# Cross-attention and expert block: another order of scores, maxima and weighings within each group

## The chip, the cores and the metric

The kernel runs on one core of one Trainium2 chip. The metric is device time of one execution in microseconds, the median of several runs. Before the change three runs gave 823.15 us in the median (822.39 to 824.36).

## The reference

The input is `x` (4 batches, 512 tokens, 256 channels) and a context of 4 x 1024 tokens. Three things are computed:

```
x = x + cross_attention(layernorm(x), context, context, mask)   # 16 heads of 16 channels, rope on q and k,
                                                                # scores / 4, masked keys -10000, softmax, @ w_o.T
x = x + ffn(layernorm(x)), where ffn is
    h + attention over the 4 batch entries of a token (causal softmax, 4 kv heads), then
    + sum over the top 2 of 8 experts of gate * (gelu(y @ w1) @ w2), y = layernorm(h)
```

The change touches only the first of these, the cross-attention: for each batch and head, 512 queries against 1024 keys, `softmax(q k / 4) v`.

## The kernel before

The program has three blocks, one after the other: cross-attention (`cross_attention`), the second attention with routing (`second_block`), and the experts (`experts_block`). Only the order of work in the first is changed.

The cross-attention is cut into 16 *quads* (four heads of one batch) and each quad into 8 *key tiles* of 128 keys. A quad and a key tile make a *group*; there are 128 groups. What a group has to do:

- four *scores* S0 to S3 (L966), one for each head: a matmul of 128 keys by 512 queries into a bank. ScalarE takes the exponential of each (L616) into a buffer of probabilities;
- one *weighing* (L981): four heads' probabilities times the values, which add up in the bank `values` over the 8 key tiles. The weighing of group g-1 stands inside group g;
- some *maxima* for the next quad (L928, then VectorE's reduction L757). The softmax subtracts a maximum of each query row, so the scores are computed once before with queries as rows, two matmuls of 512 columns each into a *wide* slot, and reduced by VectorE. A quad has 16 of them, spread over some 7 groups of the quad before, so a group has two in most cases, sometimes one or three or none;
- *jobs*: `nm` (VectorE puts a quad's 16 maxima together), `mxt` (TensorE turns them, L933, ScalarE copies them to `mxp`, L610, and SyncE moves them into the query stack by DMA, L387, so that the score matmul subtracts them), `xn` and `xT` (the normalised input of the next batch and its transpose), `q`, `k`, `v` (projections), `rope` and `c` (GpSimd), `out` (transpose of a quad's weighed sum and division, L938), `oT` and `oP` (transpose and output projection).

`attention_order` gives every job and maximum a time; the whole part of the time is its group. `steps_of` (L91) then writes out the order within each group, and each engine goes through that one list and takes what is its own. So the list sets the program order of TensorE, ScalarE and VectorE at once. From group 116 on (`g >= late`) there are no maxima, and the list is another.

Two rings hold the results of TensorE. Scores, `q`, `k`, `v` and `mxt` take three banks (`narrow`) in turn, by L280: a score waits for the exponential (or the copy) of the third one before it in that ring. Maxima, `xT`, `out`, `oT` and `oP` take two wide slots in turn: each waits until VectorE is through with the one before the last. A weighing waits for all four exponentials of its group:

```
pe.wait_ge(exp_done, 4 * g + 4)
```

An engine carries out its list in order. What waits holds up all that stands behind it on its engine.

The heads of a quad lie in pairs: S0 and S2 use rows 0 to 63 of the array, S1 and S3 rows 64 to 127 (`r = HALF * (hq % 2)`). Of a maximum's two matmuls, the first uses rows 64 to 127 and the second rows 0 to 63.

Of the kernel before, what the change touches and what calls it, by code (L numbers as in the profile page):

```python
# [35 lines left out]
def lead(quad):  # L36
    return 3 + 0.25 * max(quad - 5, 0)
# [8 lines left out]
def attention_order():  # L46
# [12 lines left out]
    for t in range(1, B):  # L59
        g = 32 * (t - 1)  # L60
        timed += [(g + 5.8, ("xn", t)), (g + 7, ("xT", t)), (g + 8.5, ("q", t, 0)), (g + 10, ("q", t, 1)), (g + 10, ("rope", t, 2))]
        timed += [(g + x, ("v", t, n // 2, n % 2)) for n, x in enumerate((11.5, 13.5, 15, 16.5))]
    for t in range(2, B):
        g = 32 * (t - 2)
# [5 lines left out]
    for b in range(B - 1):  # L70
        g = 32 * b + 32
# [5 lines left out]
    def when(g):  # L77
        return begins[int(g)] + (g - int(g)) * lengths[int(g)]
# [5 lines left out]
    for quad in range(1, QUADS):  # L84
        first, last = when(max(8 * (quad - 1) - lead(quad - 1), 0)), when(8 * quad - lead(quad))
# [5 lines left out]
    def steps_of(g):  # L91

        here = [j for t, j in timed if int(t) == g]
        tops, rest = [[j for j in here if (j[0] in ("max", "nm")) == is_max] for is_max in (True, False)]
        if g >= late:
            return [("job", ("pair", g)), ("score", 4 * g + 2), ("score", 4 * g + 3), ("weigh", g - 1)] + [("job", j) for j in rest]
        first, later = rest[:1], rest[1:]
        early = tops[:1] if len(tops) > 2 else []
        tops = tops[len(early):]
        steps = [("score", 4 * g)] + [("job", j) for j in early + first] + [("score", 4 * g + 1)] + [("job", j) for j in tops[:1]] + [("score", 4 * g + 2)]  # L100
        steps += [("weigh", g - 1)] * (g > 0) + [("score", 4 * g + 3)]
        for n in range(max(len(tops) - 1, len(later))):
            steps += [("job", j) for j in tops[1 + n:2 + n] + later[n:n + 1]]
        return steps

    steps = [steps_of(g) for g in range(GROUPS)]
    after = [("moments", 0), ("warm", GROUPS), ("out", QUADS - 1), ("warm", GROUPS + 1), ("oT1", B - 1), ("warm", GROUPS + 2), ("oP1", B - 1, 0), ("tile0", 0), ("oP1", B - 1, 1), ("warm", GROUPS + 3)]
    after += [("root0", 0), ("again0", 0), ("root0", 1), ("rates0", 0)]
# [1835 lines left out]
```

## Time and profile before

| | |
|---|---|
| median of three runs | 823.15 us |
| the profiled execution, first to last instruction | 808.3 us |
| TensorE matmul busy | 706.0 us (87%) |
| VectorE busy | 557.3 us (69%) |
| ScalarE busy | 485.6 us (60%) |
| GpSimd busy | 355.8 us (44%) |
| exponentials (L616), of one score each | 488, mean 601 ns |
| reductions of maxima (L757) | 256, mean 1223 ns |

The profile is of one execution, so its span and the median of the runs are not the same thing; launch and end lie outside the span. "Busy" counts a matmul from its start to its modelled end, so that two matmuls in different halves of the array overlap and a TensorE that is busy 87% of the time can still be short of its peak. In the rows further down a time is microseconds from the start of the span. The timeline puts equal instructions that follow each other into one row (x2, x8); its start is that of the first.

### The profile page before, as it was taken

How to read it: one execution, taken by the hardware profiler on the slowest of the kernel's cores; microseconds unless marked ns; L12 is line 12 of the kernel's file. 1: busy time of each engine (PE TensorE's matmuls, PEld its weight loads, DVE VectorE, ACT ScalarE, POOL GpSimd, SP SyncE). 2: the span in 40 equal slices, each digit the busy share in tenths (PEclk: the TensorE clock that was granted, in tenths of full speed). 3: DMA queues.
4: the chain of work that ended last, by engine and by line, in shares of the span. 5: the costliest groups of instructions: out<-in, count | busy, mean ns of one | idle time of the engine just before them, and what ended most of it. 6: DMA issues, size and time to landing. Idle time of an engine off the chain costs nothing. (4 is left out here: it accounts for less than half of the span.)

```text
span 808.3 us, 13262 instructions
## 1 busy us (share of the span) xinstructions
PE 706.0 (87%) x4318; PEld 425.8 (53%) x4318; DVE 557.3 (69%) x924; ACT 485.6 (60%) x940; POOL 355.8 (44%) x262
## 2 busy tenths in 40 slices
PE   3246899999899999899999899888978889999996
PEld 2242434443344443435334333276767778999986
DVE  5949777778777778778878884248996515555553
ACT  2010556777576778567766678856655136676673
POOL 4964605358006277005749991000035723544444
PEclk9775689999999999999989999999998799999999
DMA  9676264868655666114777872039925646633321
GB/s 258 213 224 165 84 240 124 229 155 271 206 158 173 176 187 239 58 45 119 224 260 262 276 273 79 1 93 358 344 53 135 256 108 141 120 35 40 33 32 20
DMA packets 59718, 130.71 MB, mean 162 GB/s; under 512 B 8869, under 2 KB 26309, under 8 KB 58197
## 3 DMA queue, kind: packets, MB, share of 16 engines
q1 hardware_dynamic: 33364, 72.86, 27.6%
q0 software_dynamic: 16848, 35.95, 17.6%
q10 hardware_dynamic: 9440, 21.06, 9.0%
q8 instruction: 37, 0.61, 0.3%
q14 instruction: 29, 0.23, 0.1%
HBM read 80.80 MB, written 69.39 MB: 186 GB/s over the span
## 5 line engine op out<-in xcount | busy, mean ns | idle before, releaser
L757 DVE TENSOR_REDUCE mx<-wide 128x2 f32<-128x1024 f32 x256 | 305.6, 1223 | 89.0 <-PE wide L928 88.4
L616 ACT ACTIVATE probs<-narrow 128x512 f32<-128x512 f32 x488 | 267.3, 601 | 94.4 <-PE narrow L966 92.6
L966 PE MATMUL narrow<-qst,kst 51*128 51x512 f32 x488 | 182.9, 464 | 4.2 <-ACT probs L616 3.5
L928 PE MATMUL wide<-kst,qst 49*128 49x512 f32 x512 | 159.7, 476 | 21.4 <-DVE mx L757 9.4
L966 PEld LDWEIGHTS narrow<-qst,kst 51*128 51x128 f32 x488 | 78.9, 190 | 147.3 <-ACT probs L616 94.7
L981 PE MATMUL values<-probs,vaug 128*17 128x512 f32 x1024 | 139.2, 616 | 1.4 <-ACT probs L616 0.8
L1735 POOL DMA_INDIRECT out<-res,token x39 | 61.2, 1569 | 91.7 <-DMA out<-res,token 60.2
L928 PEld LDWEIGHTS wide<-kst,qst 49*128 49x128 f32 x512 | 68.6, 198 | 43.7 <-DVE mx L757 28.0
L462 POOL TENSOR_TENSOR turn_b<-turn_a,tab 128x1024 f32<-128x1024 f32 x10 | 24.2, 2420 | 115.3 <-ACT turn_a L610 114.8
L1267 POOL DMA_DIRECT2D out<-xt x4 | 5.5, 1376 | 108.1 <-DVE xt L1462 108.1
L1760 ACT ACTIVATE h_hi<-narrow 128x512 fp32r<-128x512 f32 x39 | 23.3, 598 | 42.2 <-PE narrow L1840 42.2
L1786 DVE TENSOR_TENSOR h_lo<-narrow,h_hi 128x512 fp32r<-128x512 f32 x39 | 27.0, 692 | 23.3 <-ACT h_hi L1760 23.3
L1274 POOL DMA_INDIRECT list_rows<-lists,rows_to x32 | 32.2, 1008 | 17.9 <-DVE rows_to L1532 9.1
L981 PEld LDWEIGHTS values<-probs,vaug 128*17 128x17 f32 x1024 | 17.1, 96 | 42.9 <-issue 27.6
L457 POOL TENSOR_SCALAR keep<-keep 128x512 f32<-128x512 int32 x7 | 13.7, 1960 | 52.9 <-ACT turn_a L610 42.8
L1782 DVE TENSOR_TENSOR y_lo<-y_full,y_hi 128x256 fp32r<-128x256 f32 x39 | 16.6, 426 | 29.0 <-ACT y_hi L1747 29.0
L1747 ACT ACTIVATE y_hi<-wide,lncol 128x128 fp32r<-128x128 f32 x78 | 36.3, 465 | 0.0
L1746 ACT ACTIVATE y_full<-wide,lncol 128x128 f32<-128x128 f32 x78 | 35.8, 459 | 0.1
L610 ACT ACTIVATE vaug<-narrow 128x512 f32<-128x512 f32 x16 | 9.6, 599 | 34.5 <-PE narrow L828 34.5
L1831 PE MATMUL wide<-w_hi,y_hi 128*128 x78 | 28.2, 442 | 0.1
L1591 PE MATMUL narrow<-ident 128*128 128x128 f32 x172 | 24.9, 314 | 3.7 <-PEq L1900 2.1
L610 ACT ACTIVATE mxp<-narrow 8x512 f32<-8x512 f32 x16 | 9.3, 580 | 30.9 <-PE narrow L933 30.8
(281 smaller groups left out, 1310.4 us busy)
## 6 DMA issues: line engine op xcount, KB each, us to landing
list_rows<-in_w ACTq DMA_DIRECT2D x56, 342.0 KB, 5.5
kst<-k_pieces SPq DMA_DIRECT2D x14, 784.0 KB
k_pieces<-turn_a SPq DMA_DIRECT2D x16, 512.0 KB, 5.2
w_hi<-w_hi SPq DMA_DIRECT2D x16, 512.0 KB, 11.0
w_lo<-w_lo SPq DMA_DIRECT2D x16, 512.0 KB, 11.8
turn_a<-in_w POOLq DMA_DIRECT2D x11, 512.0 KB, 5.7
w_hi<-turn_b POOLq DMA_DIRECT2D x11, 512.0 KB, 3.0
w_lo<-turn_a POOLq DMA_DIRECT2D x11, 512.0 KB, 4.6
```

Source lines behind the costliest of these rows:

```text
L616: nc.scalar.activation(probs[:, n % NP, :], score_bank(n), ACT.Exp, scale=DK ** -0.5).then_inc(exp_done, 1)
L757: last = nc.vector.tensor_reduce(mx[quad % 2][:, qt, :, hp, kh], slot[:, :, :], axis=AX.X, op=ALU.max)
L928: last = nc.tensor.matmul(slot[:, i, :], qst[u % 3][r:r + R_MAX, h, P * qt:P * qt + P], kst[u % 3][r:r + R_MAX, h, 512 * kh:512 * kh + 512 ...
L966: nc.tensor.matmul(score_bank(n), kst[u % 3][r:r + R_ALL, h, P * kt:P * kt + P], qst[u % 3][r:r + R_ALL, h, :], start=True, stop=True).the ...
L981: last = nc.tensor.matmul(values[32 * hq:32 * hq + DK + 1, :], vaug[b % 2][:, kt, h, :], probs[:, (4 * g + hq) % NP, :], start=kt == 0, st ...
L1274: pool.indirect_dma_start(list_dram, bass.IndirectOffsetOnAxis(rows_to[:, j, i, s:s + 1], 0), lists[j][:, i, s, :].bitcast(U32), None).the ...
L1591: nc.tensor.matmul(bank[:, 0:P], ident[:, :], ident[:, :], start=True, stop=True)
L1735: pool.indirect_dma_start(out, bass.IndirectOffsetOnAxis(token[:, n:n + 1], 0), res[n % PIECES][:, :], None, bounds_check=TOKENS - 1, oob_ ...
L1746: nc.scalar.activation(yT[n % 2][:, k, :], y_banks[n % 2][:, k, :], ACT.Identity, **affine)
L1747: last = nc.scalar.activation(yT_hi[n % 2][:, k, :], y_banks[n % 2][:, k, :], ACT.Identity, **affine)
L1786: nc.vector.tensor_tensor(hT_lo[n % 2][:, :, :], h_banks[n % 2], hT_hi[n % 2][:, :, :].bitcast(F32), ALU.subtract).then_inc(h_lo_set, 1)
L1831: last = nc.tensor.matmul(up_banks[n % 2], a[n % 2][:, k, :], w[:, bass.ds(e, 1), k, :].rearrange("p e n -> p (e n)"), start=(i, k) == (0, ...
```

## The change

```
-        tops, rest = [[j for j in here if (j[0] in ("max", "nm")) == is_max] for is_max in (True, False)]
+        tops, rest = [[j for j in here if (j[0] == "max") == is_max] for is_max in (True, False)]
         if g >= late:
             return [("job", ("pair", g)), ("score", 4 * g + 2), ("score", 4 * g + 3), ("weigh", g - 1)] + [("job", j) for j in rest]
-        first, later = rest[:1], rest[1:]
-        early = tops[:1] if len(tops) > 2 else []
-        tops = tops[len(early):]
-        steps = [("score", 4 * g)] + [("job", j) for j in early + first] + [("score", 4 * g + 1)] + [("job", j) for j in tops[:1]] + [("score", 4 * g + 2)]
-        steps += [("weigh", g - 1)] * (g > 0) + [("score", 4 * g + 3)]
-        for n in range(max(len(tops) - 1, len(later))):
-            steps += [("job", j) for j in tops[1 + n:2 + n] + later[n:n + 1]]
-        return steps
+        steps = [("score", 4 * g)] + [("job", j) for j in tops[:1]] + [("score", 4 * g + 1)] + [("weigh", g - 1)] * (g > 0)
+        steps += [("score", 4 * g + 2)] + [("job", j) for j in tops[1:2]] + [("score", 4 * g + 3)]
+        return steps + [("job", j) for j in tops[2:] + rest]
```

Before, a group was: S0, (a first maximum if there are three), the first job, S1, a maximum, S2, the weighing of the group before, S3, then what is left of maxima and jobs in turn. Now it is: S0, a maximum, S1, the weighing, S2, a maximum, S3, a third maximum if there is one, then all jobs. `nm` counts as a job now and no longer as a maximum. Five lines fewer: what is L966 before is L961 after, and so on.

The next rows are TensorE's program order at three places. The numbers behind names are those of the buffers: `narrow0` to `narrow2` are the banks of the score ring, `wide0` and `wide1` the wide slots.

First a place without jobs, from the weighing of group 84 to that of group 85. Before:

```order
L981 MATMUL values<-probs,vaug0 17x512 x4
L966 MATMUL narrow2<-qst2,kst2 128x512
L928 MATMUL wide1<-kst0,qst0 128x512 x2
L966 MATMUL narrow0<-qst2,kst2 128x512
L966 MATMUL narrow1<-qst2,kst2 128x512
L928 MATMUL wide0<-kst0,qst0 128x512 x2
L966 MATMUL narrow2<-qst2,kst2 128x512
L981 MATMUL values<-probs,vaug0 17x512 x4
```

Now:

```order
L976 MATMUL values<-probs,vaug0 17x512 x4
L961 MATMUL narrow1<-qst2,kst2 128x512
L923 MATMUL wide1<-kst0,qst0 128x512 x2
L961 MATMUL narrow2<-qst2,kst2 128x512
L961 MATMUL narrow0<-qst2,kst2 128x512
L923 MATMUL wide0<-kst0,qst0 128x512 x2
L961 MATMUL narrow1<-qst2,kst2 128x512
L976 MATMUL values<-probs,vaug0 17x512 x4
```

The kinds stand in the same row; only the banks differ. Before, the scores between two weighings are S3, S0, S1, S2, and the weighing needs the exponential of the first of them. Now they are S2, S3, S0, S1, and the weighing needs the exponential of the second.

Then the `mxt` of quad 4, a job of group 29. Before, it stands between the weighings of groups 27 and 28:

```order
L981 MATMUL values<-probs,vaug0 17x512 x4
L966 MATMUL narrow2<-qst1,kst1 128x512
L966 MATMUL narrow0<-qst1,kst1 128x512
L933 MATMUL narrow1<-ident,mh0 8x128 x4
L966 MATMUL narrow2<-qst1,kst1 128x512
L928 MATMUL wide1<-kst2,qst2 128x512 x2
L966 MATMUL narrow0<-qst1,kst1 128x512
L981 MATMUL values<-probs,vaug0 17x512 x4
```

Now it stands between those of groups 28 and 29:

```order
L976 MATMUL values<-probs,vaug0 17x512 x4
L961 MATMUL narrow2<-qst1,kst1 128x512
L923 MATMUL wide0<-kst2,qst2 128x512 x2
L961 MATMUL narrow0<-qst1,kst1 128x512
L928 MATMUL narrow1<-ident,mh0 8x128 x4
L961 MATMUL narrow2<-qst1,kst1 128x512
L923 MATMUL wide1<-kst2,qst2 128x512 x2
L961 MATMUL narrow0<-qst1,kst1 128x512
L976 MATMUL values<-probs,vaug0 17x512 x4
```

It has moved by one weighing. The same holds for every job that was the first of its group.

Last the `out` of quad 6, a job of group 57, which has three maxima. Before, between the weighings of groups 55 and 56:

```order
L981 MATMUL values<-probs,vaug1 17x512 x4
L966 MATMUL narrow1<-qst0,kst0 128x512
L966 MATMUL narrow2<-qst0,kst0 128x512
L928 MATMUL wide0<-kst1,qst1 128x512 x2
L938 MATMUL wide1<-ident,outT 128x128 x4
L966 MATMUL narrow0<-qst0,kst0 128x512
L928 MATMUL wide0<-kst1,qst1 128x512 x2
L966 MATMUL narrow1<-qst0,kst0 128x512
L981 MATMUL values<-probs,vaug1 17x512 x4
```

Now, between those of groups 56 and 57:

```order
L976 MATMUL values<-probs,vaug1 17x512 x4
L961 MATMUL narrow1<-qst0,kst0 128x512
L923 MATMUL wide1<-kst1,qst1 128x512 x2
L961 MATMUL narrow2<-qst0,kst0 128x512
L923 MATMUL wide0<-kst1,qst1 128x512 x2
L933 MATMUL wide1<-ident,outT 128x128 x4
L961 MATMUL narrow0<-qst0,kst0 128x512
L923 MATMUL wide0<-kst1,qst1 128x512 x2
L961 MATMUL narrow1<-qst0,kst0 128x512
L976 MATMUL values<-probs,vaug1 17x512 x4
```

Two maxima stand ahead of `out` and one behind it, where before there were one and one.

## Rows read from the trace of the kernel before

**Rows 1.** First line of the page.

```profile
span 808.3 us, 13262 instructions
```

**Rows 2.** Stage windows: length, each engine's busy us, clock, DMA share, GB/s.

```profile
88.00:492.00 404.00, 379.38 (x2287) 164.18 (x2287) 315.87 (x329) 281.45 (x517) 204.76 (x146) 0.97 0.59 188
492.00:527.00 35.00, 32.40 (x210) 11.64 (x207) 7.97 (x31) 29.94 (x50) 0.00 (x0) 1.00 0.01 2
```

**Rows 3.** Waits from 88 to 492 us: us in total, times, longest.

```profile
PEld narrow L966 <- ACT probs L616: 91.8, 149, 1.8
```

**Rows 4.** TensorE's timeline, a plain group: start, us, instruction.

```profile
388.30 0.50 PE L966 MATMUL narrow<-qst,kst 51*128 51x512 f32 x1
388.30 0.72 PE L928 MATMUL wide<-kst,qst 49*128 49x512 f32 x2
...
389.48 0.50 PE L966 MATMUL narrow<-qst,kst 51*128 51x512 f32 x1
389.91 1.05 PE L981 MATMUL values<-probs,vaug 128*17 128x512 f32 x8
390.90 0.50 PE L966 MATMUL narrow<-qst,kst 51*128 51x512 f32 x2
```

**Rows 5.** ScalarE and VectorE in the same group; the page's row of L616.

```profile
388.83 1.08 ACT L616 ACTIVATE probs<-narrow 128x512 f32<-128x512 f32 x2 [0.81 <-PE narrow L966]
...
389.07 2.36 DVE L757 TENSOR_REDUCE mx<-wide 128x2 f32<-128x1024 f32 x2 [0.65 <-PE wide L928]
...
L616 ACT ACTIVATE probs<-narrow 128x512 f32<-128x512 f32 x488 | 267.3, 601 | 94.4 <-PE narrow L966 92.6
```

**Rows 6.** TensorE's timeline at two mxt jobs.

```profile
308.56 0.60 PE L933 MATMUL narrow<-ident,mh 128*8 128x128 f32 x4 [0.86 <-DVE mh L767]
309.08 0.50 PE L966 MATMUL narrow<-qst,kst 51*128 51x512 f32 x1
...
392.50 1.05 PE L981 MATMUL values<-probs,vaug 128*17 128x512 f32 x8
...
395.58 1.05 PE L981 MATMUL values<-probs,vaug 128*17 128x512 f32 x8
```

**Rows 7.** TensorE's timeline at an xT job.

```profile
347.70 1.09 PE L915 MATMUL wide<-ident,attn 128*128 128x128 f32 x8 [1.16 <-DVE mx L757]
```

**Rows 8.** TensorE's timeline: weighings around two out jobs (L938).

```profile
383.61 1.05 PE L981 MATMUL values<-probs,vaug 128*17 128x512 f32 x8
...
387.31 1.05 PE L981 MATMUL values<-probs,vaug 128*17 128x512 f32 x8
...
405.94 1.05 PE L981 MATMUL values<-probs,vaug 128*17 128x512 f32 x8
...
408.99 0.66 PE L938 MATMUL wide<-ident,outT 128*128 128x128 f32 x4 [0.96 <-DVE mx L757]
...
410.79 0.62 PE L981 MATMUL values<-probs,vaug 128*17 128x512 f32 x4
```

**Rows 9.** TensorE's timeline: weighings around an oP job.

```profile
327.54 1.05 PE L981 MATMUL values<-probs,vaug 128*17 128x512 f32 x8
...
333.59 0.62 PE L981 MATMUL values<-probs,vaug 128*17 128x512 f32 x4
```

**Rows 10.** Timelines: mxp of quads 4 and 2, first score of each.

```profile
194.81 0.59 ACT L610 ACTIVATE mxp<-narrow 8x512 f32<-8x512 f32 x1
...
202.91 0.50 PE L966 MATMUL narrow<-qst,kst 51*128 51x512 f32 x2 [0.64 <-DMA qst<-mxp]
...
143.61 0.59 ACT L610 ACTIVATE mxp<-narrow 8x512 f32<-8x512 f32 x1 [0.16 <-PE narrow L933]
...
149.94 0.40 PE L966 MATMUL narrow<-qst,kst 51*128 51x512 f32 x1
```

**Rows 11.** All mh operations of nm: duration ns min/median/max.

```profile
L767 DVE TENSOR_TENSOR mh<-nm,mh x16: 175/176/1799, 79.6 to 494.0; 128x16 fp32r<-128x16 f32 x16
```

**Rows 12.** Window of half clock: length, busy us, clock, DMA share, GB/s.

```profile
216.80:220.20 3.40, 3.40 (x19) 2.52 (x21) 1.38 (x3) 0.47 (x1) 0.00 (x0) 0.50 0.02 6
```

## Prediction

> **What bounds the kernel now.** I read the page first: the span is 808.3 us [rows 1], and the median of the three timed runs is 823.15 us, so 14.85 us lie outside the span; I add every change to the span of this one execution and keep the 14.85. The stage windows come next: from 88 to 492 us, 404 us long, run the 116 groups whose order the change rewrites, and TensorE is busy for 379 of them; the twelve late groups (492 to 527 us) and the two later blocks keep their order [rows 2]. The waits of this stretch are led, on TensorE's side, by scores waiting for an exponential, 91.8 us in 149 waits [rows 3]: TensorE is nearly full, and what it still waits for is ScalarE.
>
> The timeline of one plain group shows why. I count in intervals, from one weighing (L981) to the next. From 388.30 the score S3 and one of the two matmuls of a maximum start together, S0 and S1 follow, S2 starts only at 389.48, the weighing at 389.91, the next score at 390.90: 2.60 us [rows 4]. The exponential of S3 starts at 388.83 and takes 0.60 (601 ns is the mean of one); its end, 389.43, plus 0.05 is the start of S2 [rows 4, 5]. So 2.60 = 0.53 (score to exponential) + 0.60 + 0.05 + 0.43 (S2 to weighing) + 0.99 (weighing to the next score). It is a loop through one exponential, not TensorE's work, and VectorE's two maxima, 2.36 of the 2.60 us, just fit in it [rows 5].
>
> **The change, part by part.** The instructions are the same; only their order changes. I listed both orders interval by interval, for weighings 4 to 111 (108 intervals), and priced each kind by the distance between the two weighing rows around it in before, as shown for the kinds below. The two half-clock stretches of before are taken as falling again at the same cost.
>
> *Plain intervals.* The cycle of scores and maxima is as before, but the weighing stands one score earlier in it. It needs the exponential of S3, now issued as the second score after the last weighing, not the first. Two exponentials in a row take 1.08 us from the first start to the second end [rows 5]. The loop is therefore 0.53 + 1.08 + 0.05 + 0.99 = 2.65 to 2.66, against 2.60: I take +0.07. S1, held by S2's exponential, starts 1.18 after S2 and would allow the weighing at 1.61; the second exponential, at 1.66, ends last. 49 intervals hold no job where before 43 did (six jobs moved in with others); 45 of the 49 are plain in this sense: 45 x 0.07 = **+3.2**. In every eighth ScalarE's copy of the weighed sum delays the exponential of S2, which used not to be waited for, by 0.09 (my estimate; it can be 0 to 0.2): **+0.9**. Early intervals behind the xn job and in half clock: **+0.7**. Bounds of all three together: 0 and +8.
>
> *The turned maxima (mxt).* An mxt that waits for nothing makes the interval 3.08 (392.50 to 395.58), 0.49 over 2.59; the one at 308.56 has TensorE idle 0.86 for VectorE's mh, since nm stands right ahead of it [rows 6]. The 14 mxt intervals of before, read in the same way, hold 11.0 us over 2.59 each. Now no mxt follows nm within an interval, so that wait goes; eight stand alone (8 x 0.49) and six share an interval with a k, v or oP job, where they cost the 0.52 from mxt to the next score [rows 6]: 7.0 us. **-4.0**, bounds -6 and -1.
>
> *q, k, v, xT.* Same price, bound by TensorE (in both orders two pairs of starts stand ahead of the job and two behind it). Slightly more have three maxima beside them (+0.24 each): **+0.9**. xT used to wait 1.16 us for a maximum straight behind the four xn operations [rows 7]; it now stands an interval further: **-1.0** for the three. Bounds of both together -3 and +3.
>
> *out.* This is the expensive one. It takes a wide slot, so the maximum behind it waits for the reduction of the one ahead. With two maxima in the interval it takes 3.70 (383.61 to 387.31), with three 4.85 (405.94 to 410.79, TensorE idle 0.96 for a reduction) [rows 8]. All maxima of a group now go ahead of its jobs, and in groups 57 and 65 that puts three into out's interval, as in 89 and 97: 4 instead of 2. What they leave are intervals with one maximum, which are not shorter than 2.66, because the loop above holds them. 2 x 1.15, plus 0.6 for the one out of quad 2 that had a single maximum: **+2.9**, bounds 0 and +4.
>
> *oT and oP.* An oP with three maxima behind an oT waits twice for reductions and takes 6.05 (327.54 to 333.59) [rows 9]. Laid out by the same waits, the three batches go different ways: in the first an oP loses its cheap place beside a group with few maxima (+1.15), in the second one gets rid of a third maximum (-1.15), and in the third nm no longer stands between two maxima that oP waits for (-0.6). **-0.6**, bounds -4 and +4.
>
> *The transfer of the maxima rows.* mxt of quad 4 moves from the head of group 29 to its end, one interval, while the scores of group 32 that need it do not move. Before, mxp starts at 194.81 and the score waits until 202.91, 8.10 us after mxp and already 0.64 idle [rows 10]. Now TensorE comes back about 5.0 us after mxp. If the transfer is as slow, it waits 3.1 us; if it is as fast as for quad 2, whose score started 6.33 us after mxp without a wait (143.61 to 149.94), at most 1.3 [rows 10]. The store of key pieces ahead of it in SP's queue moves by the same interval, so I take near the slow end: 2.6 us in place of 0.65, **+2.0**, bounds -0.6 and +2.6. The other quads do not wait in before, and I expect none to: where the room is smallest (quads 2, 3, 5, 7) mxt was already the last job of its group and does not move.
>
> The last intervals (112 on) come out even: out and the last mxt each move one interval, and the weighing before them is cheaper by as much. Weighings 0 to 3 are even too, since the same twelve maxima are spread differently.
>
> Sum: 3.2 + 0.9 + 0.7 - 4.0 + 0.9 - 1.0 + 2.9 - 0.6 + 2.0 = **+5.0 us**; the span goes from 808.3 to 813.3, the time from 823.15 to **828.2**.
>
> nm itself: its last operation takes 0.18 us in the median and once 1.80 [rows 11]. The page "SBUF — State Buffer" of the Trainium skill, section "SBUF: two separate sides", says that a VectorE operation with two SBUF inputs and a GpSimd one that reads SBUF lock each other out of a shared port pair; the trace agrees in so far as the 1.80 us are ten times the median of the same instruction. By that rule such a delay can fall on any nm of the new order as well; the sum has none of it either way.
>
> **Rivals.**
> *A, the losses do not come (822.8).* The two half-clock stretches of before may be children of its order: in the first, from 216.8 to 220.2, the granted clock is 0.50 (1.2 of 2.4 GHz) [rows 12], right behind the oP that waited. By my estimate from the same kinds of intervals in full clock they cost 1.4 and 2.0 us. Without them and with the transfer in time: 828.2 - 3.4 - 2.0 = 822.8. For it: an oP that loses its waits; against: oP and out have as many waits as before.
>
> *B, clearly faster (815.6).* If the array started matmuls strictly in program order, the old order would pay one more start of 0.23 us than the new one, since its score S3 and the first matmul of the maximum use the same half of the rows and the new S2 does not. In the 54 or so intervals that are full of work this gives 828.2 - 54 x 0.23 = 815.8, with a little of the plain ones 815.6. Against it: the rows show a maximum's matmul starting at 388.30 together with S3, so it already passes its elder [rows 4]. The page "TensorE: Matmul & The Clock Gate", section "Part 3: Packing small matmuls — row/col tiling", of the Trainium skill states that matmuls are strictly first in, first out. By that rule B would hold; the trace disagrees, and I give it little.
>
> *C, well slower (832).* One mechanism: the idle stretch ahead of the score of group 32. At 3 us it is longer than any of the waits for ScalarE in before, 1.8 at most [rows 3], and if the clock falls to half behind it, as behind the oP, it costs another 1.4 us, and a second quad whose mxt also moves to the end of its group (quad 8, where the key pieces of the next batch are stored too) waits about as long as quad 4 here beyond the forecast, 1.0 to 2.4. It decides from the point where the rows land later than 5 us after mxp. 828.2 + 1.4 + 2.4 = 832.0.
>
> *D, still plain.* If a second exponential is not in the loop, 3.2 us go and the time is 825.0; this stays inside the forecast's own range, 825 to 831.
>
> **How the numbers follow.** The forecast (with D) gets 0.58, A 0.18, B 0.07, C 0.17. About 0.2% is what a measurement of this kernel can tell from no change: 821.5 to 824.8. Faster: B and a third of A, 0.13. Same: the rest of A and the low edge of the forecast, 0.17. Slower: 0.70. The range 821.5 to 833.0 leaves out B and the far part of C.
>
> **What would show it right or wrong.** Right: plain intervals of 2.66 with the weighing, not S2, waiting for ScalarE; four out intervals of 4.85; a wait for the rows' transfer ahead of group 32 of 2 us or more; mxt with no wait for mh. Wrong: plain intervals of 2.60 or less, weighings that do not wait, the score of group 32 waiting under 1 us, or intervals with v or k at 3.7 (then B). If the stage from 88 to 527 us does not grow by about 5 us, the forecast is wrong even if the total agrees.

## The result and the profile after

| | before | changed |
|---|---|---|
| median of 15 runs | 821.77 us (813.98 to 828.67) | 827.76 us (821.67 to 830.70) |
| ratio, 95% interval | | 1.0072 (1.0050 to 1.0095) |
| profiled execution: span | 808.3 us | 827.6 us |
| weighing 3 to weighing 111 in it | 380.7 us | 390.1 us |

The kernel became slower by 6.0 us; 5.0 were forecast. The two spans differ by 19.3 us, and that is not the change. In every run of the changed kernel the time is 1.8 to 2.1 us above the span (829.6 and 827.6 in the profiled one), so the 14.85 us "outside the span" of the forecast's first paragraph was a mistake: the profile before must be of an execution of some 810 us, and should have been read so. The forecast added its sum to the time as well as to the span, so this did not move it. The stage windows of the changed kernel (length, busy us of PE, PEld, DVE, ACT, POOL, clock, DMA share, GB/s) answer to [rows 2]:

```profile
88.80:498.00 409.20, 378.86 (x2292) 164.85 (x2292) 317.69 (x329) 278.37 (x519) 204.87 (x146) 0.97 0.58 183
...
607.50:683.70 76.20, 54.60 (x350) 49.23 (x350) 32.83 (x157) 22.73 (x42) 35.09 (x34) 0.80 0.48 143
```

TensorE is as busy as before (378.9 against 379.4 us in the groups); the stage is longer by waiting. From the first score to the last weighing it takes 442.1 us here and 441.1 in a second execution of the changed kernel, against 438.5, 436.0 and 436.6 in three of before: 4.6 us more in the mean, about what the forecast asked of this stage. The last row is a stage behind the attention, the lists for the experts. It took 64.6 us in the profile before and does not depend on the order in the first block, as the experiments show. (An interval is numbered by the weighing that ends it: interval 7 lies between weighings 6 and 7.)

A plain group, TensorE, answers to [rows 4]:

```profile
398.08 1.05 PE L976 MATMUL values<-probs,vaug 128*17 128x512 f32 x8
399.07 0.50 PE L961 MATMUL narrow<-qst,kst 51*128 51x512 f32 x1
399.07 0.73 PE L923 MATMUL wide<-kst,qst 49*128 49x512 f32 x2
...
400.25 0.50 PE L961 MATMUL narrow<-qst,kst 51*128 51x512 f32 x1
```

and ScalarE beside it:

```profile
399.60 1.09 ACT L611 ACTIVATE probs<-narrow 128x512 f32<-128x512 f32 x2 [0.59 <-PE narrow L961]
```

The next weighing starts at 400.74 (the row stands further down), 2.66 us later. Two exponentials run from 399.60 to 400.69, and 0.05 later the weighing starts. The waits of this stage (us in all, times, longest) say the same: the weighing waits for ScalarE 63 times, 20.4 us, where a later execution of the kernel before has 38 times and 11.7 us; the scores' row is little more than in [rows 3].

```profile
PEld narrow L961 <- ACT probs L611: 96.8, 152, 1.7
...
PEld values L976 <- ACT probs L611: 20.4, 63, 0.6
```

An mxt with nothing to wait for costs 3.07 to 3.09 in all eight intervals where it stands alone, [rows 6] without the wait for mh:

```profile
400.74 1.05 PE L976 MATMUL values<-probs,vaug 128*17 128x512 f32 x8
...
402.39 0.60 PE L928 MATMUL narrow<-ident,mh 128*8 128x128 f32 x4
...
403.82 1.05 PE L976 MATMUL values<-probs,vaug 128*17 128x512 f32 x8
```

Out with three maxima, [rows 8]: four intervals of 4.83, 4.83, 4.82 and 5.25 (the last in half clock), and the wait ahead of out is there, 1.08 against 0.96.

```profile
300.24 1.05 PE L976 MATMUL values<-probs,vaug 128*17 128x512 f32 x8
...
303.28 0.66 PE L933 MATMUL wide<-ident,outT 128*128 128x128 f32 x4 [1.08 <-DVE mx L752]
...
305.07 0.62 PE L976 MATMUL values<-probs,vaug 128*17 128x512 f32 x4
```

Group 32, where the forecast had a wait of 2.6 us for the maxima rows, shows none [rows 10]: mxp at 198.40, the score 4.8 us later (it is the second of the two in its row, at 203.21) and no idle time ahead of it.

```profile
198.40 0.57 ACT L605 ACTIVATE mxp<-narrow 8x512 f32<-8x512 f32 x1
...
202.98 0.62 PE L961 MATMUL narrow<-qst,kst 51*128 51x512 f32 x2
```

Two places are worse than forecast. The first score of group 8 waits for the rows of quad 1. SyncE issued their transfer at 110.54, 1.7 us after mxp had ended (108.26 + 0.57), behind two loads of the mask and one of the context. TensorE and then SyncE:

```profile
113.55 1.09 PE L910 MATMUL wide<-ident,attn 128*128 128x128 f32 x8
118.25 0.79 PE L961 MATMUL narrow<-qst,kst 51*128 51x512 f32 x1 [3.60 <-DMA qst<-mxp]
```

```profile
107.30 2.37 SPq L328 DMA_DIRECT2D keep<-in_mask  x2
109.71 0.78 SPq L321 DMA_DIRECT2D craw<-in_ctxT  x1
110.54 1.27 SPq L382 DMA_DIRECT2D qst<-mxp  x2
```

And interval 99, with oP, mxt and three maxima, takes 9.74 us. TensorE:

```profile
446.38 1.05 PE L976 MATMUL values<-probs,vaug 128*17 128x512 f32 x8
...
448.23 0.50 PE L923 MATMUL wide<-kst,qst 49*128 49x512 f32 x2 [0.38 <-DVE xT_lo L730]
...
450.74 0.50 PE L923 MATMUL wide<-kst,qst 49*128 49x512 f32 x2 [1.77 <-DVE mx L752]
451.87 0.50 PE L823 MATMUL wide<-wo_hi,xT_hi 128*128 128x256 f32 x2 [0.63 <-DVE mx L752]
...
456.11 0.62 PE L976 MATMUL values<-probs,vaug 128*17 128x512 f32 x4
```

and VectorE in the same time:

```profile
446.95 1.22 DVE L730 TENSOR_TENSOR xT_lo<-wide,xT_hi 128x1024 fp32r<-128x1024 f32 x1 [2.55 <-ACT xT_hi L605]
448.09 0.17 DVE L756 TENSOR_REDUCE nm<-mx 128x16 f32<-128x32 f32 x1
448.30 1.04 DVE L760 CAST mh<-nm 128x16 fp32r<-128x16 f32 x1
449.38 0.18 DVE L762 TENSOR_TENSOR mh<-nm,mh 128x16 fp32r<-128x16 f32 x1
449.47 3.48 DVE L752 TENSOR_REDUCE mx<-wide 128x2 f32<-128x1024 f32 x3
```

oT's copy, nm, an mh of 1.04 us and only then the three reductions: TensorE waits three times, 2.8 us in all, for that row of work. The mh of 1.04 us ended 0.04 us after an instruction of GpSimd that had begun 0.05 us ahead of it:

```profile
448.25 1.05 POOL L535 CAST turn_b<-turn_a 128x1024 fp32r<-128x1024 f32 x1
```

At both places the clock falls to half, and in two more stretches; the third begins in an interval with out and three maxima. The windows (columns as above, the clock is the last but two):

```profile
118.00:124.90 6.90, 6.65 (x23) 3.18 (x24) 3.58 (x3) 2.77 (x5) 0.00 (x0) 0.51 0.46 185
220.40:223.80 3.40, 3.40 (x18) 1.60 (x16) 1.41 (x5) 1.08 (x2) 0.00 (x0) 0.51 0.15 58
329.70:336.60 6.90, 6.90 (x27) 3.04 (x27) 2.88 (x3) 3.09 (x6) 0.00 (x0) 0.51 0.02 7
452.50:455.90 3.40, 3.40 (x17) 2.38 (x16) 1.14 (x2) 0.61 (x2) 3.31 (x5) 0.51 0.80 267
```

### The profile page after: what moved, and what is told of

The parts are those of the page before. It is cut to its first block and busy times, and to the rows that moved or that the text cites. A ratio compares the mean times of both kernels' runs of the same rounds, so it can differ in the third digit from the quotient of the medians.

```text
span 827.6 us, 13262 instructions
## 1 busy us (share of the span) xinstructions
PE 708.5 (86%) x4318; PEld 428.1 (52%) x4318; DVE 557.9 (67%) x924; ACT 481.4 (58%) x940; POOL 355.8 (43%) x262
## 5 line engine op out<-in xcount | busy, mean ns | idle before, releaser
L611 ACT ACTIVATE probs<-narrow 128x512 f32<-128x512 f32 x488 | 261.4, 601 | 90.9 <-PE narrow L961 89.8
L961 PE MATMUL narrow<-qst,kst 51*128 51x512 f32 x488 | 179.8, 458 | 10.2 <-ACT probs L611 6.1
L961 PEld LDWEIGHTS narrow<-qst,kst 51*128 51x128 f32 x488 | 77.1, 188 | 150.7 <-ACT probs L611 100.1
L976 PE MATMUL values<-probs,vaug 128*17 128x512 f32 x1024 | 137.1, 608 | 1.4 <-ACT probs L611 0.8
L923 PEld LDWEIGHTS wide<-kst,qst 49*128 49x128 f32 x512 | 70.3, 196 | 47.0 <-DVE mx L752 30.4
L457 POOL TENSOR_TENSOR turn_b<-turn_a,tab 128x1024 f32<-128x1024 f32 x10 | 24.2, 2424 | 118.6 <-ACT turn_a L605 118.0
L1269 POOL DMA_INDIRECT list_rows<-lists,rows_to x32 | 32.2, 1007 | 29.4 <-DVE rows_to L1527 20.9
L976 PEld LDWEIGHTS values<-probs,vaug 128*17 128x17 f32 x1024 | 17.1, 95 | 44.6 <-ACT probs L611 26.0
L1586 PE MATMUL narrow<-ident 128*128 128x128 f32 x172 | 26.5, 315 | 12.5 <-issue 9.1
L1586 PEld LDWEIGHTS narrow<-ident 128*128 128x128 f32 x172 | 24.9, 228 | 13.2 <-issue 11.7
```

The costliest lines, as they stand in the source:

```text
L611: nc.scalar.activation(probs[:, n % NP, :], score_bank(n), ACT.Exp, scale=DK ** -0.5).then_inc(exp_done, 1)
L923: last = nc.tensor.matmul(slot[:, i, :], qst[u % 3][r:r + R_MAX, h, P * qt:P * qt + P], kst[u % 3][r:r + R_MAX, h, 512 * kh:512 * kh + 512 ...
L961: nc.tensor.matmul(score_bank(n), kst[u % 3][r:r + R_ALL, h, P * kt:P * kt + P], qst[u % 3][r:r + R_ALL, h, :], start=True, stop=True).the ...
L976: last = nc.tensor.matmul(values[32 * hq:32 * hq + DK + 1, :], vaug[b % 2][:, kt, h, :], probs[:, (4 * g + hq) % NP, :], start=kt == 0, st ...
L1269: pool.indirect_dma_start(list_dram, bass.IndirectOffsetOnAxis(rows_to[:, j, i, s:s + 1], 0), lists[j][:, i, s, :].bitcast(U32), None).the ...
L1586: nc.tensor.matmul(bank[:, 0:P], ident[:, :], ident[:, :], start=True, stop=True)
```

## The experiments

Twelve kernels ran in three sets of four, each set on another chip and each kernel beside the kernel before. The medians of before in the three sets were 810.6, 819.4 and 819.4 us, so only ratios are compared across sets. The first set is before again, weighing back, weighing early and changed with out relieved; the second is changed again, old cycle, old cycle relieved and rows earlier; the third is the rest. "Stage" is weighing 3 to weighing 111 in the profile. An interval is plain if it holds no job; the column gives those with two maxima.

| kernel | ratio to before (95%) | stage, us | plain interval | k with two maxima |
|---|---|---|---|---|
| before, again | 0.9974 (0.9945 to 1.0004) | 378.2 | 2.59 to 2.60 | 3.92 |
| before, third | 1.0015 (0.9985 to 1.0044) | 381.3 | 2.59 to 2.60 | 3.92 |
| changed, again | 1.0124 (1.0099 to 1.0150) | 385.6 | 2.65 to 2.66 | 3.90 |
| weighing back | 1.0240 (1.0190 to 1.0289) | 401.7 | 2.83 | 4.42 |
| weighing early | 1.0223 (1.0181 to 1.0265) | 396.4 | 2.83 | 4.42 |
| old cycle | 1.0286 (1.0260 to 1.0312) | 396.3 | 2.59 to 2.60 | 4.43 |
| jobs early | 1.0222 (1.0170 to 1.0273) | 397.0 | 2.65 to 2.66 | 4.43 |
| rows earlier | 1.0146 (1.0103 to 1.0189) | 384.3 | 2.65 to 2.66 | 3.90 |
| changed, out relieved | 0.9971 (0.9937 to 1.0005) | 380.5 | 2.65 to 2.66 | 3.90 |
| old cycle, relieved | 1.0124 (1.0097 to 1.0151) | 387.7 | 2.59 to 2.60 | 4.42 |
| before, relieved | 1.0066 (1.0027 to 1.0105) | 378.5 | 2.59 to 2.60 | 3.92 |
| changed, relieved | 0.9975 (0.9946 to 1.0004) | 374.6 | 2.65 to 2.66 | 3.90 |

### Where do 19 us of span come from? Before, again and third

No edit. 

> The kernel before once more, unchanged, for a second profile of it. Question: the profiled executions of before and after differ by 19.3 us in span, the medians of the timed runs by 6.0. Theory 1 (the later blocks differ from execution to execution, whatever the order in the first): the ratio is 1.000 within 0.3%, the attention stage (first score to last weighing) is again within 2 us of before's 439, and the stage behind it lies anywhere from 282 to 297 us, the idle time of TensorE in it being what differs. Rival (the new order lengthens the later blocks): the stage behind the attention stays within 1 us of 282.5.

> The kernel before a third time, unchanged. Question: in four kernels (the changed one, twice, and three variants) the stage from the first to the last list of expert rows takes 61 us and the next one starts 76 to 77 us after it began; in the kernel before (twice) and three others it takes 49 to 50 and 64 to 66 us. Theory 1 (this belongs to the chip or the hour, not to the order in the first block): the kernels of this call all have the same stage length, be it 65 or 76 us, whatever their order. Rival (the new order brings it): the two kernels with the old order here have 65, the two with the new one 76.

The stage of the lists, from the first list of expert rows to the first expert: 64.8 us in the second execution of before, 76.1 in the third. The kernels of the first set all had 64 to 66 us, those of the second and third set all 76 to 78, old order or new. So it belongs to the chip or the hour, and 11.6 of the 19.3 us were that. The third execution of before:

```profile
600.90:677.00 76.10, 53.71 (x350) 48.22 (x350) 32.84 (x157) 22.79 (x42) 35.17 (x34) 0.82 0.49 143
```

TensorE is busy for 53.7 us here and 54.6 in the changed kernel's profile, against 49.6 and 51.1 in the two short ones, at a granted clock of 0.82 and 0.80 against 0.87 and 0.84; and in the changed kernel's profile 9.1 us of its idle time there are put down to "issue", to nothing that the profile shows. What it is stays open.

The two executions also give the stage of the old order three times: 380.7, 378.2, 381.3. And the score of group 32 waited in neither of the new ones; the 0.64 of [rows 10] was that one execution's.

### The changed kernel, again

No edit. 

> The changed kernel once more, unchanged, on the chip on which the other comparisons run and for a second profile. Theory 1 (the extra time of the attention stage is in the order: plain intervals 2.65, four out intervals of 4.83, the wait for the maxima rows ahead of group 8 and the half clock behind it): ratio to before 1.005 to 1.010, attention stage (weighing 3 to 111) 386 to 391 us against 378 to 381. Rival (the 9 us of the first profile were mostly half-clock stretches that fell there by chance): the same classes of intervals at full clock, but the stage within 3 us of before's and a ratio of 1.000 to 1.004.

The first theory holds in its intervals; the ratio lies above its 1.010. On this chip the loss is larger, 1.0124, 9.8 us and twice the forecast. The classes of intervals are those of the first profile to 0.02 us, but for an oP (5.26 against 4.84). What differs beside it is what comes by chance: this execution stood at half clock until 103.2 us, reached group 8 only when the rows had landed (no wait), and had 13.7 us of half clock in the stage where the first had 20.4.

### The weighing, back and early

```
 # changed kernel, weighing behind S2              # kernel before, weighing ahead of S2
-S0 | M | S1 | W | S2 | M | S3 | rest              -S0 | job | S1 | M | S2 | W | S3 | M
+S0 | M | S1 | S2 | W | M | S3 | rest              +S0 | job | S1 | M | W | S2 | S3 | M
```

> The changed kernel with one thing undone: the weighing stands behind the third score again; maxima, nm and jobs stay where the change put them. Theory 1 (loop through two exponentials): plain intervals fall from 2.65 to 2.59 or 2.60, the wait of the weighing for ScalarE goes to the third score, every eighth falls from 2.75 to 2.59; intervals with v, k, q, out stay. 45 x 0.06 + 13 x 0.10 = 4 us less than the changed kernel: 823.8, about +2 over before (ratio 1.002). Rival (the time comes from where maxima and jobs stand or from stretches at half clock, the weighing is hidden): plain intervals stay at 2.65 and the time stays at 827 to 828 (ratio 1.007).

> The kernel before with one thing of the change alone: the weighing stands one score earlier, ahead of the third score; all maxima and jobs stay. Theory 1: plain intervals (43 without a job) go from 2.60 to 2.65, those behind the take-out copy to 2.75 where they hold no job, mxt, k, v, q and out unchanged: +2.5 to +4, so 825 (ratio 1.004). Rival (weighing hidden): 821.8, ratio 1.000, plain intervals 2.60.

Both expectations failed where an interval holds two maxima, 2.59 and 2.65 against 2.83 in each, and the kernels are among the slowest. Where it holds one, they came true: with the weighing back 14 of 19 such intervals take 2.58 to 2.60, with the weighing early six of eight take 2.65 to 2.66. So the loops are as expected, and the place of a maximum beside the weighing is what was left out (in the two intervals of each kernel with 2.81 to 2.82 the only maximum stands there too). The timeline of a group with two maxima and the weighing back shows why:

```profile
324.52 1.05 PE L976 MATMUL values<-probs,vaug 128*17 128x512 f32 x8
325.50 0.49 PE L923 MATMUL wide<-kst,qst 49*128 49x512 f32 x2
325.83 0.40 PE L961 MATMUL narrow<-qst,kst 51*128 51x512 f32 x2
...
326.92 0.50 PE L961 MATMUL narrow<-qst,kst 51*128 51x512 f32 x1 [0.21 <-ACT probs L611]
327.35 0.62 PE L976 MATMUL values<-probs,vaug 128*17 128x512 f32 x4
```

The loop is there, but its first link is longer: the maximum now stands first behind the weighing, its two matmuls use both halves of the rows, and S3 starts 1.31 instead of 0.98 behind the weighing. 1.31 + 0.43 + 0.60 + 0.06 + 0.43 = 2.83. With the weighing early it is the other end:

```profile
325.26 1.05 PE L981 MATMUL values<-probs,vaug 128*17 128x512 f32 x8
...
327.43 0.50 PE L966 MATMUL narrow<-qst,kst 51*128 51x512 f32 x1 [0.21 <-ACT probs L616]
327.44 0.73 PE L928 MATMUL wide<-kst,qst 49*128 49x512 f32 x2
328.10 0.62 PE L981 MATMUL values<-probs,vaug 128*17 128x512 f32 x4
```

The score that waits for the exponential starts 2.17 behind the weighing, and a maximum behind it needs two more starts, so 0.67 pass to the next weighing instead of 0.43. Each single edit of this cycle is worse than both whole orders: a score has to be first behind the weighing and a score last ahead of it, and the change kept that, with other scores.

### The old cycle with the new place of the jobs

```
-S0 | M | S1 | W | S2 | M | S3 | rest
+S0 | S1 | M | S2 | W | S3 | M | rest
```

> The changed kernel with the cycle of scores, maxima and weighing of the kernel before (S0 S1 M S2 W S3 M), but nm and all jobs behind them, as the change has it. The two single edits before it showed that an interval's length is set by which instruction stands first behind the weighing and last ahead of it; here both are scores again, S3 and S2. Theory 1 (loop weighing, S3, its exponential, S2, weighing): plain 2.59 to 2.60 in all 45, none of the 2.83 of the single edits; mxt stands behind a maximum again and costs 3.34 instead of 3.08 (8 times, +2.0); k, v, q as in the changed kernel: about 1.5 to 3 us less than the changed kernel, ratio to before 1.003 to 1.006. Rival (jobs all at the end of the group are what makes the long intervals, whatever the cycle): plain at 2.8 as in the single edits, ratio 1.02.

Plain intervals go back to 2.59, nm and jobs standing as in the changed kernel: the 0.06 is the loop through the second exponential. But the kernel is 13 us slower than the changed one, since k and v take 4.43 instead of 3.90 (19 intervals with three maxima among them, 0.5 each, and four with q) and mxt 3.35 instead of 3.08, of which I had expected only the latter. TensorE's starts around a k of this kernel:

```profile
162.50 1.05 PE L976 MATMUL values<-probs,vaug 128*17 128x512 f32 x8
163.49 0.49 PE L961 MATMUL narrow<-qst,kst 51*128 51x512 f32 x1
163.49 0.72 PE L923 MATMUL wide<-kst,qst 49*128 49x512 f32 x2
164.15 0.73 PE L823 MATMUL narrow<-c_hi,wk_hi 128*128 128x512 f32 x2
...
165.74 0.50 PE L961 MATMUL narrow<-qst,kst 51*128 51x512 f32 x2
166.08 0.40 PE L923 MATMUL wide<-kst,qst 49*128 49x512 f32 x2
166.50 0.50 PE L961 MATMUL narrow<-qst,kst 51*128 51x512 f32 x1
166.93 0.63 PE L976 MATMUL values<-probs,vaug 128*17 128x512 f32 x4
```

A job of 128 rows starts beside nothing. Ahead of it stand S3 and M, in the upper half of the rows twice and in the lower half once, so two starts; behind it S0, S1, M, S2, lower half three times, so three. The changed kernel has S2, M, S3 ahead and S0, M, S1 behind, two starts each. That halves are what counts is my reading of the program's rows and the times; the profile does not name the halves. It fits both single edits too: with the weighing back three starts stand behind a late job, with the weighing early three ahead of an early one, and k takes 4.41 to 4.43 in both.

### The jobs early in the new cycle

```
-S0 | M | S1 | W | S2 | M | S3 | nm, jobs
+S0 | job | M | S1 | W | S2 | M | S3 | nm, mxt
```

> The changed kernel with the first job of a group (q, k, v, xT, out, oT, oP) between S0 and the maximum behind it, where the kernel before had it; mxt and nm stay at the end, weighing and maxima stay. This is the fourth of four combinations of cycle and place of the jobs. k with two maxima is 3.92 with the old cycle and early jobs, 4.43 with the old cycle and late jobs, 3.90 with the new cycle and late jobs. Theory 1 (a job costs 0.5 more where it parts two instructions that would start as a pair in different halves of the array): here it parts S0 and the first matmul of a maximum: 4.4 in the 17 intervals with q, k, v: +8 us on the changed kernel, ratio 1.017 to 1.022. Rival (a job costs the same anywhere in the new cycle): ratio 1.010 to 1.012, k 3.90.

It holds: 4.41 to 4.44 in the five k, ratio 1.0222. Ahead of the job stand S2, M, S3, S0: lower half three times. With this the four combinations are: k with two maxima 3.92 (old cycle, early job), 4.43 (old, late), 3.90 (new, late), 4.43 (new, early). So place and cycle belong together, and the change moved both by what keeps them paired. The kernel before has one case of its own: the v of interval 45, the second job of its group, stands ahead of S0 and takes 4.44 in all three executions, where the other v with two maxima take 3.88 to 3.94. With the weighing early its count is even, and it alone among the v takes 3.88. I had not seen this when I wrote that both orders have two pairs of starts on either side of every job.

### The third maximum beside out

```
+    for g, to in ((57, 56), (65, 64), (89, 90), (97, 98)):   # one maximum of group g to group `to`
```

> The changed kernel with four maxima moved by one group: out of groups 57, 65, 89 and 97, which hold out and three maxima, into the neighbour that has only one. Theory 1 (three maxima beside out cost two waits for a reduction): these four intervals fall from 4.83 (one 5.25) to 3.70, the neighbours stay at 2.65 with two maxima instead of one: -4.6 us, 823.2 (ratio 1.002). Rival (a maximum costs VectorE's 1.22 us wherever it stands, since VectorE is nearly full): the neighbours grow by about 1 us each, the sum is 0 and the time 827 to 828.

All 13 out intervals are 3.68 to 3.71. Of the four neighbours that took a maximum in, three stay as they were (2.66, and 2.75 twice, where ScalarE also takes a weighed sum out); the fourth holds an xT, where a second maximum costs 0.60 (3.09 to 3.69). So the intervals give 3.9 us, not 4.6. The stage is 380.5 against 385.6 and 390.1 of the changed kernel, and the ratio to before 0.9971 against 1.0072 and 1.0124, on different chips: 8 to 13 us, of which the four moved maxima explain only the 3.9.

### Twelve maxima moved, in three orders

```
+    for g, to in ((11, 12), (23, 24), (35, 36), (47, 46), (50, 51), (53, 52),
+                  (57, 56), (65, 64), (69, 70), (77, 78), (89, 90), (97, 98)):
```

> The cycle of the kernel before, nm and jobs behind it, and twelve maxima moved by one group, out of groups with three maxima and a job into neighbours with one or none. Theory 1: out 3.70 in all 13 (4 x 1.13 saved against three maxima), k, v and oP 0.24 to 1 less in eight, plain 2.60 with two maxima as with one: 6 to 8 us under the same kernel without the moves, ratio to before 0.995 to 0.998. Rival (VectorE, busy 2.45 of 2.60 us in a plain interval, has no room for the moved maxima): intervals that take one in grow, ratio 1.003 or more.

> The kernel before with the same twelve maxima moved by one group, out of groups with three and a job into neighbours with one or none (nm no longer counts when a third maximum is looked for). Jobs keep their place between S0 and S1. Theory 1 (plain 2.60 holds two maxima as well as one, a third one costs 1.13 beside out and 0.24 beside k or v): -2 x 1.13 + 0.6 for the out that had one, -1.0 for four k and v, -0.5 to -2 for the oP: 3 to 5 us under before, ratio 0.994 to 0.997, k and v at 3.92, not the 4.43 they have at a group's end with this cycle. Rival (VectorE has no room): ratio 1.000 or more, plain intervals with two maxima over 2.60.

> The changed kernel with the same twelve maxima moved. Theory 1: out 3.70 in all 13, k and v 3.90 where they lose the third maximum, plain 2.65, mxt 3.08: 6 to 8 us under the changed kernel, within 2 us of before, ratio 0.998 to 1.002. Against the kernel with these moves and the old cycle, jobs at the group's end (829.5, ratio 1.012): k and v 0.52 less in 17 intervals, mxt 0.27 less in 8, plain 0.06 more in 46, so 8 us less. Rival (the cycle does not matter for the jobs): ratio 1.010.

With the old cycle and late jobs the expectation failed as above (k and v at 4.42). The moves themselves took 12.5 us off the same kernel without them (842.0 to 829.5), more than the 6 to 8 expected; of the plain intervals that took a maximum in, seven stay as they were, and two grow, to 2.88 and 3.06. With before's order the ratio is 1.0066, slower, though outs are at 3.71: nm now often stands behind a maximum and right ahead of mxt, and two such intervals take 4.98 and 5.18 instead of 3.33 and 4.20, and an xT with a third maximum 5.79 instead of 4.66. Even so its stage is 2.8 us shorter than that of before in the same set, with as much half clock, so the loss is not in that profile. The timed runs show where it is at least in part: the granted clock is 0.934 in the mean of its twelve runs and 0.940 in the 29 of before, 9 us more at half clock (3 to 4 us of time, at the price estimated below), while the profiled run had 0.942. With the changed order the time is as expected, though two plain intervals that took a maximum in grow to 2.83 and 3.27: stage 374.6, 11.0 under the changed kernel's second profile (some 4 of them by half clock, 3.4 us of it against 13.7), ratio 0.9975. Against the changed kernel's 1.0124 beside the same median of before that is 1.5% less. The old cycle with the same moves and late jobs has 1.0124 too, so the rival, that the cycle does not matter, is out. No version was shown faster than before: the upper ends of this one and of the one with four moves are 1.0004 and 1.0005.

```profile
294.30 1.05 PE L983 MATMUL values<-probs,vaug 128*17 128x512 f32 x8
...
295.94 0.66 PE L940 MATMUL wide<-ident,outT 128*128 128x128 f32 x4
...
297.99 1.05 PE L983 MATMUL values<-probs,vaug 128*17 128x512 f32 x8
```

The out that waited 1.08 does not wait here.

### The rows of quad 1 earlier

```
-AHEAD = 4                                      +AHEAD = 6
-    return 3 + 0.25 * max(quad - 5, 0)         +    return 4 if quad == 1 else 3 + 0.25 * max(quad - 5, 0)
```

> The changed kernel with the maxima rows of quad 1 ready one group earlier: two more of its maxima ahead of the first group, mxt of quad 1 in group 4 instead of 5. In the first profile of the changed kernel the first score of group 8 stood idle 3.9 us for that transfer (9.99 us after mxp), and the clock was at half for 6.8 us from the moment it started. Theory 1 (the idle time brings the half clock): the wait falls to about 1.2 us, no half-clock stretch between 110 and 130 us, intervals 7 and 8 together 8 to 9 us instead of 14.1; the start grows by 0 to 2.4 us for the two maxima; net -2 to -5 us on the changed kernel. Rival (the rows land when the transfers of the next batch ahead of them are through, at about 118 us, whenever mxp is): the wait is as long, gap 12.6 us instead of 10, nothing gained, half clock as before.

Inconclusive. The score of group 8 did not wait, but neither did it in the changed kernel of the same set, and the start grew by 5.1 us (88.3 to 93.4). In four profiles of the new order with the rows at their old time (the two unchanged ones, four moves, twelve moves) this score waits 3.60, 0, 2.27 and 1.42 us; in none of the three of before does it wait. It waits 0.60 in before with twelve moves, though, where SyncE issued the transfer 2.9 us after mxp began. In the four executions with a wait the rows landed 28.6 to 29.6 us after the first score of all, with mxp 18.9 to 20.9 us after it. That speaks for the rival, that the loads of the next batch ahead of this transfer set its time, and does not show it.

## Why the prediction was right, and where not

| term | forecast | measured | from |
|---|---|---|---|
| plain, take-out, early | +4.8 | +4.1 | 45 x 0.06, seven at 2.75 instead of 2.65; early ones +0.6 (3.04 and 2.84) |
| mxt | -4.0 | -3.4 | 8 x 3.08; shared ones +0.5, one +1.1 |
| q, k, v, xT | -0.1 | -1.7 | sums of their intervals; xT alone -1.8 |
| out | +2.9 | +2.8 | 49.8 to 52.8 us, 0.2 of it half clock |
| oT, oP | -0.6 | +2.2 | third batch |
| rows' transfer | +2.0 | 0 to +3.6 | quad 1, not quad 4 |

The measured column is the second profile of the changed kernel against the second of before, less what I estimate for half clock: one stretch of 3.4 us costs 1.2 to 1.5 us, read from intervals 57 and 58 (5.02 + 5.25 against 4.83 + 3.90) and 66 (4.89 against 3.70). Its first five rows add up to +4.0; the two stages differ by 7.4 us, 3.9 of them outside half clock.

**Right.** The main mechanism was the forecast's: the loop through two exponentials, 2.65 to 2.66 with the weighing as the one that waits, and the old cycle put back into the changed kernel brings 2.59. So was the largest loss that I had forecast beside it, out with three maxima, which moving four maxima took away. Rival B is out: k and v stayed at 3.9, and TensorE's starts pair as I had counted them. D is out too, its 2.60 did not come, and so is A: the half clock of the old order did not go away, it moved and did not shrink.

**The step that failed: the transfer of the maxima rows.** I put the wait at group 32, from one row of 0.64. Two more executions of before and all of the new order have no wait there. The rows were late for group 8 instead, where I had written that the other quads would not wait. Quad 1's mxt moved by one interval too, and where the score before started 9.9 us after mxp, TensorE now comes back after 6.4 (118.25 less the 3.60 of idle time, less 108.26), while the rows took 10.0, 8.6, 7.8 and at most 6.3 us in four executions. Quad 1 had not looked tight, because I read its room from before and not from the new order. Nor had I counted what SyncE issues ahead of the rows; here it issued them 1.7 us late. Rival C's mechanism is what happened there, at another quad: 3.60 us idle, and half clock from 118.0, just as TensorE started again (118.25). It cost 5.1 us against the same two intervals of the next profile (14.1 and 9.0).

**The third oP batch** was sized with waits for reductions alone. What I had missed is VectorE's row: with nm a job behind oT, oT's copy, nm and both mh stand ahead of three reductions, and one of the mh took 1.04. The forecast left long mh out of its sum on both sides, and judged them by the last mh operation alone, where the first of the two is the one that is often long. In all fourteen profiled executions together 120 of the 448 mh operations took over 0.20 us, and 118 of these ended 0.03 to 0.04 us after an instruction of GpSimd.

**Half clock** was taken as equal on both sides. In the stage the three profiles of the old order hold 11.6, 4.7 and 10.2 us of it, the two unchanged ones of the new order 20.4 and 13.7. Less 1.35 for each 3.4, the old order needs 376.1 to 377.3 us, the new one 382.0 and 380.2: in the mean 4.5 us more at full clock and 3.3 more by the clock. Counted from the first score on, which takes in the start, the five hold about as much on either side (27.3, 20.5 and 17.1 us against 20.5 and 23.9). The timed runs decide it for the second set: the changed kernel's six were granted 0.934 of the full clock in the mean and the eleven of before beside them 0.941, with standard errors of 0.001. That is some 109 and 97 us at half clock in an execution, and by the same price 5 of the 9.8 us of loss there; in which stages it fell is not on record. All five profiles of the new order with late jobs, relieved or not, have a stretch right at interval 99; two of the three of before have none within 20 us of it. That an idle TensorE is what brings it is what these places suggest. The twelve moves, which only spread maxima, raised the clock of the old cycle from 0.935 to 0.941 within one set, and lowered that of before from 0.940 to 0.934, where they brought new waits; but no experiment took idle time away and left all else.

Range and sign held, and the time is 1.0 us from the forecast, but on the next chip it would have been 4.8 from it. The total agrees better than its parts, and that is luck: 0.7 too much in the plain intervals, 1.6 in q to xT and 2.0 for a transfer that waited elsewhere or not at all stand against 0.6 too little in mxt, 2.8 in oP and what the clock took.

## What to carry to other kernels

Where an engine with two halves is full, count starts by halves between two instructions that use the whole: an odd one cost 0.5 us here, and all six orders fit that count. Where a loop through another engine bounds the cycle, its first and last link count: the instruction that feeds the loop has to be first behind the fence and the one that it releases last ahead of the next. And a third of something that a slot allows twice should be moved into a neighbour with room before anything else is tuned; here that won back what the change had lost. A neighbour with a job of its own has no such room (xT + 0.60).

## What the runs showed of the hardware

- The second matmul of a maximum starts ahead of the first where the halves ask for it: in the kernel before S3 (upper half) and the second matmul (lower half) start within 7 ns of each other, the first 0.33 us later (388.295, 388.302 and 388.636 us; the second is the one that carries the signal to VectorE). VectorE's reduction, at 389.07, starts only when both have ended.
- The first mh operation, of 128 x 16, took 174 ns at best, 387 in the median and 1347 at most in the changed kernel's profile. Over all fourteen profiles the 249 mh operations of either kind that ran with no instruction of GpSimd beside them took 174 to 182 ns but for two; of the 199 with one, 118 took over 200 ns, and 2364 at most.
- The same stage took 64 to 66 us in one set and 76 to 78 in two others, whatever the kernel, with 3 to 5 us more of TensorE's busy time in the long ones. A span and a time of different executions should not be subtracted.
